# A three-layer interaction tower on one core: chunk 1's transfers on ScalarE's queue, the context product first, the last layer 2 in another bank

## The chip, the cores and the metric

The program runs on one core of a Trainium2 chip. The time is the device time of one execution in microseconds; three executions of the kernel before took 659.74, 657.54 and 658.29 us, so the median is 658.29 us. The engines are TensorE (PE in the profile; PEld is its weight load), VectorE (DVE), ScalarE (ACT), GpSimd (POOL) and SyncE (SP), which issues most DMA transfers.

## The reference

39 embedding tables are looked up for 512 samples, which gives e with 39 fields of 16 numbers for each sample. Three interaction layers follow, and then a small dense network on their outputs and on 16 context numbers:

```python
x0 = inputs; xk = inputs                       # (512, 39, 16)
for idx, (W, b) in enumerate(params):          # W: (39, fields of xk, 128)
    z = jnp.einsum('bhd,bkd,hks->bsd', x0, xk, W) + b[None, :, None]
    z = jax.nn.relu(z)
    if idx != n_layers - 1:
        half = z.shape[1] // 2
        xk = z[:, :half, :]; direct.append(z[:, half:, :])
    else:
        direct.append(z)
logit = jnp.sum(jnp.concatenate(direct, axis=1), axis=-1)      # (512, 256)
h = jnp.concatenate([logit, dense_ctx], axis=1)
h = jnp.maximum(h @ W_top1 + b_top1, 0.0)      # 272 -> 512
h = jnp.maximum(h @ W_top2 + b_top2, 0.0)      # 512 -> 256, then W_top3: 256 -> 1
```

## The kernel before

The 512 samples are cut into 16 chunks of 32 (`NCH`), so a chunk has N = 32 * 16 = 512 columns. For each chunk and layer, VectorE multiplies pairs of field rows (a product tile, `prod`, of 128 partitions and 2 x 512 numbers), and TensorE multiplies it with the weights and sums up in one PSUM bank: `z0` for layer 0 (written L0 here), `z1` for layer 1 (L1), `z2` for layer 2 (L2). L0 has 4 such groups in a chunk, L1 and L2 have 10 each.

Some groups are taken in two parts (`SPLIT`): ScalarE rounds the product to a short format (`high`), and the rest (`low`) is formed by GpSimd or, for the four groups in `THROUGH_PSUM`, by VectorE. TensorE then runs three cheaper passes (`sum_high`, `sum_low`) in place of the full-precision one (`sum_whole`).

The order is written out by hand. Stage i does L0 of chunk i, the first groups of L2 of chunk i-1, L1 of chunk i, and the rest of L2 of chunk i-1; a last stage (i = NCH) does L2 of chunk 15. Each engine runs its own list in order, and semaphores join the lists.

How a chunk's data comes in: GpSimd gathers its rows from the table (`gather`), 10 indirect DMAs for each chunk. Two copies of the gathered rows are stored to `x0_rows` in DRAM (`store_x0`); a DRAM to DRAM copy makes five more (`repeat_x0`); from there `x0base` (the second factor of L0, which ScalarE copies to the PSUM bank `base`), `spread0` (the first factors of L0) and three pieces of `spread` (the first factors of L1 and L2) are loaded. All of this is on SP's queue, except part of chunk 0's, which is on ScalarE's. The names `L261`, `L264` (stores), `L272` (repeat), `L283` (x0base), `L298` (spread0) and `L314` (spread) are those lines. The queue is one list: chunk 0's three spread loads are issued ahead of chunk 1's stores.

When a layer's sums are done, ScalarE takes relu of them out of the PSUM bank into `x1` or `x2` in the two arrangements that the next layer's products need (`copies`: six instructions, L464), and the other half of the rows into `r01` (L488, L502) or `r2` (L509), which VectorE reduces to the logits. For chunk 0 alone the copies are shared by ScalarE and VectorE (`first_copies`, four instructions on each, L472 and L616).

At the end, TensorE first does the context rows' product for the 512 hidden units (four matmuls, L763) ahead of the last stage, into `h1_sum`, whose first part is `z0`; after the last stage the logits' products are added to it (L769, L772), and ScalarE takes relu with the bias (L556). The second dense layer (L778), its relu (L560), the last product into `z0` (L783), a copy (L563) and the output transfer follow.

Of the kernel before, what the change touches and what calls it, by code (L numbers as in the profile page):

```python
# [8 lines left out]
P = 128  # L9
# [18 lines left out]
COPIES = 7  # L28

# [119 lines left out]
def tower_kernel(nc, ids, offsets, table, w0a, w0b, w1, w1_split, w2, w2_split, biases, wt1, bt1, wt2, bt2, wt3, ctxT, out):  # L149
    with ExitStack() as ctx:  # L150
# [45 lines left out]
        y_sb = sb("y_sb", [1, B])  # L196
        h1 = spread0[:, 0:H1 // P, :]
# [8 lines left out]
        h1_sum = (z0, x1[:, 0, :], x1[:, 1, :], z1)  # L206
        h2_sum = (base, x2[:, 0, :])

# [5 lines left out]
        bias_in = sem("bias_in")  # L214
        top_in = sem("top_in")
# [25 lines left out]
        h1_done = sem("h1_done")  # L241
        h1_ready = sem("h1_ready")
# [9 lines left out]
        def _(sp):  # L252
# [68 lines left out]
            sp.dma_start(bias_sb[:, :], biases).then_inc(bias_in, 16)  # L321
            sp.dma_start(w1_part, w1_split).then_inc(w1_in, 16)
# [33 lines left out]
            sp.wait_ge(y_ready, 1)  # L356
# [44 lines left out]
        def _(act):  # L401
# [4 lines left out]
            def store_first_again():  # L406

                act.wait_ge(gathered[0], 16 * GAT)
                first = x0_dram[0, F:F + 1, 0:1]
                act.dma_start(bass.AP(first.tensor, first.offset, [[D, P], [FPT * N, GAT - 1], [1, D]]),  # L410
                              gat[:, 0, 0:GAT - 1, :]).then_inc(x0_stored[0], 16)
                tail = x0_dram[0, F + FPT * (GAT - 1):F + FPT * (GAT - 1) + 1, 0:1]
                act.dma_start(bass.AP(tail.tensor, tail.offset, [[D, LAST], [1, D]]),
                              gat[0:LAST, 0, GAT - 1, :]).then_inc(x0_stored[0], 16)
# [52 lines left out]
            def first_copies(to, z, kind, layer, ready):  # L467

                act.wait_ge(mm_done, stage_end(0, kind))
# [35 lines left out]
            def relu2(c):  # L505
# [3 lines left out]
                act.activation(r2[:, :], z2[:, :], ACT.Relu, bias=bias_sb[:, 2:3]).then_inc(r2_ready, 1)  # L509
# [8 lines left out]
            store_first_again()  # L518
            load_first()
            take_base(0)  # L520
            for i in range(NCH + 1):
                if i >= 2:
                    for part in range(3):
                        relu1(i - 1, part)
                if i == NCH:
                    relu2(NCH - 2)
                for c, kind, gs in stages_of(i):
                    for g in gs:
# [6 lines left out]
                        if i == 1 and kind == "L0" and g == 1:  # L535
                            first_copies(x2, z1, "L1", 1, x2_ready)
                            relu1(0, 2)
                        if kind == "L0" and g == G0 - 1 and i >= 2:
                            relu2(i - 2)
# [13 lines left out]
            act.wait_ge(top_in, 16 * 7)  # L553
            for m in range(H1 // P):
                act.wait_ge(h1_done, m + 1)
# [297 lines left out]
```

## Time and profile before

| What | us |
|---|---|
| median of three executions | 658.29 |
| the profiled execution: time / span | 657.38 / 655.5 |
| PE busy | 608.5 (93%) |
| DVE busy | 550.0 (84%) |
| POOL busy | 537.1 (82%) |
| ACT busy | 409.3 (62%) |

The span is from the first to the last instruction of the profiled execution; 1.9 us lie around it. Stages 2 to 14 repeat every 36.35 us or so. The head (to about 80 us) and the tail (from about 610 us) are where the engines are seen waiting. "Idle before" in a row is the time in which the engine did nothing ahead of it, and the arrow names what ended that. A DMA row's duration is how long its queue took to issue it, not how long the bytes took.

### The profile page before, as it was taken

Reading aid. Unit: us, or ns where it says so; the run is one execution under the profiler, and the core shown is the slowest. Engines: PE = TensorE matmul, PEld = TensorE weight load, DVE = VectorE, ACT = ScalarE, POOL = GpSimd, SP = SyncE. Lnnn points to the kernel's source line nnn. Section 1 sums busy time; section 2 is a strip of 40 time slices with the busy share of each in tenths; the row PEclk is TensorE's granted clock in tenths of the full one; section 3 lists DMA queues with packets and bytes.
Section 4 is the critical chain, followed back from the end, with each engine's and each line's share of the span. In section 5 each row is a group of like instructions: output and inputs, shape, how many; then the busy total and the mean of one; then the engine's idle time right before and its main releaser. Section 6 shows DMA issues by size and latency. Waiting matters only on the chain.

```text
span 655.5 us, 6276 instructions
## 1 busy us (share of the span) xinstructions
PE 608.5 (93%) x1996; PEld 376.1 (57%) x1996; DVE 550.0 (84%) x620; ACT 409.3 (62%) x551; POOL 537.1 (82%) x325
## 2 busy tenths in 40 slices
PE   0178899999999999999999999999999999999998
PEld 0035466656666566656666566666566665655563
DVE  0376899898989898998989898999989898969750
ACT  2043758677676758576766757586776667584622
POOL 6786799898989899998989998999989895746530
PEclk9979899999999999999999999999999999999999
DMA  6687883838363645648374645547383745420000
GB/s 221 150 180 222 173 249 77 250 76 248 70 209 85 167 127 130 197 82 245 71 229 91 188 90 153 160 111 216 76 250 67 213 93 176 102 64 1 0 0 0
DMA packets 64043, 90.29 MB, mean 138 GB/s; under 512 B 46624, under 2 KB 49568, under 8 KB 60042
## 3 DMA queue, kind: packets, MB, share of 16 engines
q1 hardware_dynamic: 57402, 87.89, 49.5%
q0 software_dynamic: 5120, 1.29, 2.0%
q10 hardware_dynamic: 1488, 0.72, 0.4%
q8 instruction: 15, 0.25, 0.2%
q14 instruction: 18, 0.15, 0.1%
HBM read 87.31 MB, written 8.95 MB: 147 GB/s over the span
## 4 chain that ended last, share of the span: by engine, by line
PE 40%; POOL 36%; ACT 10%; issue 6%; DVE 5%; DMA 2%; SPq 0%; ACTq 0%; DVEq 0%
POOL low L378 29%; PE z L701 21%; PE z L718 10%; POOL gat L368 7%; PE z L733 6%; ACT x L464 6%; ACT high L444 2%; DVE prod L607 2%; ACT r L488 1%; DMA spread<-x_rows 1%; DVE x L616 1%; DVE prod L588 1%; DVE base L642 1%; DVE low L650 1%; PE x L778 1%
## 5 line engine op out<-in xcount | busy, mean ns | idle before, releaser
L378 POOL TENSOR_TENSOR low<-prod,high 128x1024 fp32r<-128x1024 f32 (+1 forms) x160 | 380.9, 2398 | 56.4 <-ACT high L444 55.1
L607 DVE TENSOR_TENSOR prod<-spread,x 128x1024 f32<-128x1024 f32 x256 | 308.1, 1214 | 35.3 <-ACT x L464 33.6
L701 PE MATMUL z<-prod,w_sb 128*128 128x512 f32 (+2 forms) x608 | 290.6, 598 | 37.3 <-DVE prod L588 32.8
L444 ACT ACTIVATE high<-prod 128x1024 fp32r<-128x1024 f32 (+1 forms) x160 | 167.8, 1058 | 124.0 <-DVE prod L607 99.8
L718 PE MATMUL z<-high,high_w_L 128*128 128x512 f32 (+1 forms) x448 | 203.7, 455 | 4.0 <-ACT high L444 2.8
L701 PEld LDWEIGHTS z<-prod,w_sb 128*128 128x128 f32 (+2 forms) x608 | 115.4, 190 | 122.8 <-issue 103.4
L368 POOL DMA_INDIRECT gat<-table_dram,index x160 | 155.5, 972 | 36.5 <-issue 33.9
L733 PE MATMUL z<-low,high_w_L 128*128 128x512 f32 (+1 forms) x448 | 182.1, 487 | 3.5 <-POOL low L378 1.9
L718 PE MATMUL z<-high,low_w_L 128*128 128x512 f32 (+1 forms) x448 | 179.0, 400 | 0.0
L464 ACT ACTIVATE x<-z,bias_sb 64x512 f32<-64x512 f32 (+1 forms) x180 | 116.3, 646 | 14.8 <-PE z L701 7.4
L733 PEld LDWEIGHTS z<-low,high_w_L 128*128 128x128 f32 (+1 forms) x448 | 82.8, 190 | 68.9 <-issue 44.7
L454 ACT ACTIVATE high<-base 128x512 fp32r<-128x512 f32 x128 | 75.5, 590 | 55.6 <-DVE base L642 55.2
L718 PEld LDWEIGHTS z<-high,high_w_L 128*128 128x128 f32 (+1 forms) x448 | 85.5, 191 | 42.2 <-issue 14.4
L718 PEld LDWEIGHTS z<-high,low_w_L 128*128 128x128 f32 (+1 forms) x448 | 85.5, 191 | 31.8 <-issue 14.2
L650 DVE TENSOR_TENSOR low<-base,high 128x512 fp32r<-128x512 f32 x128 | 87.8, 686 | 8.6 <-ACT high L454 8.3
L642 DVE TENSOR_TENSOR base<-spread,x 128x512 f32<-128x512 f32 x128 | 88.6, 692 | 2.3
L588 DVE TENSOR_TENSOR prod<-spread,base 117x1024 f32<-117x1024 f32 x64 | 65.4, 1082 | 15.0 <-DMA spread<-x_rows 8.4
L509 ACT ACTIVATE r<-z,bias_sb 128x512 f32<-128x512 f32 x16 | 11.0, 687 | 13.8 <-PE z L733 13.7
L628 DVE TENSOR_REDUCE logit<-r 128x32 f32<-128x512 f32 x16 | 10.9, 679 | 7.4 <-ACT r L509 7.4
L435 ACT ACTIVATE base<-x0base 117x512 f32<-117x512 f32 x16 | 9.6, 602 | 8.6 <-DMA x0base<-x_rows 8.2
L656 DVE TENSOR_TENSOR low_w_L<-spread,high_w_L 128x1792 fp32r<-128x1792 f32 (+1 forms) x2 | 3.7, 1888 | 10.1 <-DMA gat<-table_dram,index 10.1
L488 ACT ACTIVATE r<-z,bias_sb 64x512 f32<-64x512 f32 x16 | 11.0, 686 | 0.4
(37 smaller groups left out, 73.5 us busy)
## 6 DMA issues: line engine op xcount, KB each, us to landing
spread<-x_rows SPq DMA_DIRECT2D x15, 1792.0 KB, 7.1
spread<-x_rows SPq DMA_DIRECT2D x32, 768.0 KB, 11.0
spread<-x_rows SPq DMA_DIRECT2D x16, 1024.0 KB, 7.3
x_rows<-x_rows SPq DMA_DIRECT2D x16, 390.0 KB
x0base<-x_rows SPq DMA_DIRECT2D x47, 78.0 KB
gat<-table_dram,index POOLq DMA_INDIRECT x160, 3.7
x_rows<-gat SPq DMA_DIRECT2D x31, 72.0 KB, 2.3
wt_sb<-wt_dram SPq DMA_DIRECT2D x2, 512.0 KB, 17.4
```

The lines of the kernel that those rows point to most:

```text
L368: pool.indirect_dma_start(out=gat[0:rows, c % GBUF, j, :], out_offset=None, in_=table, in_offset=bass.IndirectOffsetOnAxis(ap=index[0:rows ...
L378: pool.tensor_tensor(low[0:rows, h, 0:k, :], prod[0:rows, slot(c, kind, g), 0:k, :], high[0:rows, h, 0:k, :].bitcast(F32), ALU.subtract).t ...
L444: act.activation(high[0:rows, split_slot(c, kind, g), 0:k, :], prod[0:rows, slot(c, kind, g), 0:k, :], ACT.Copy).then_inc(high_ready, 1)
L454: act.activation(high[0:rows, split_slot(c, kind, g), t, :], base[0:rows, :], ACT.Copy).then_inc(tile_high, 1)
L464: act.activation(to[at:end, tile, :], z[k:k + end - at, :], ACT.Relu, bias=bias_sb[k:k + end - at, layer:layer + 1]).then_inc(ready, 1)
L588: dve.tensor_tensor(prod[0:rows, slot(c, "L0", g), 0:k, :], spread0[0:rows, 2 * g:2 * g + k, :], base[0:rows, :].unsqueeze(1).to_broadcast ...
L607: dve.tensor_tensor(prod[0:rows, slot(c, kind, g), :, :], spread[0:rows, c % 2, g, :].unsqueeze(1).to_broadcast([rows, k, N]), x[0:rows, : ...
L642: dve.tensor_tensor(base[0:rows, :], spread[0:rows, c % 2, g, :], x[0:rows, t, :], ALU.mult).then_inc(tile_prod, 1)
L650: dve.tensor_tensor(low[0:rows, h, t, :], base[0:rows, :], high[0:rows, h, t, :].bitcast(F32), ALU.subtract).then_inc(tile_low, 1)
L701: last = pe.matmul(z[:, :], w[0:rows, at + j, :], prod[0:rows, slot(c, kind, g), j, :], start=g == 0 and j == 0, stop=closes and j == k - 1)
L718: pe.matmul(z[:, :], v[kind][0:rows, at + j, :], high[0:rows, h, j, :], start=g == 0 and j == 0 and v is high_w, stop=False)
L733: last = pe.matmul(z[:, :], high_w[kind][0:rows, at + j, :], low[0:rows, h, j, :], start=False, stop=closes and j == k - 1)
```

## The change

1. Chunk 1's stores, its repeat, its x0base and its spread0 load leave SP's queue and are issued by ScalarE: the two stores and the repeat ahead of ScalarE's relu copies of L0 of chunk 0, the loads behind them. `spread` of chunk 1 stays with SP.
2. The context product is TensorE's first work, into the banks of `x1` and `x2`; VectorE adds the bias and keeps the result in `ctx_part`. Its three small loads move to the front of SP's queue. At the end VectorE adds `ctx_part` to the hidden sums, and ScalarE's relu reads the result.
3. L2 of chunk 15 sums in `z0` in place of `z2`, so it need not wait until ScalarE has read chunk 14's sums; the hidden layer's first part takes `z2`.
4. The relu copies of L1 of chunk 15 are shared by ScalarE and VectorE; ScalarE's relu of chunk 14's L2 moves behind group 2 of the last stage, and VectorE's reduction of it behind group 5.
5. The dense layers' other weights are loaded in stage 4 (`TOP_AT`), not ahead of chunk 2's stores.
6. The last product is done in two halves of 256 columns in two banks, each copied on its own.

```diff
-        h1_sum = (z0, x1[:, 0, :], x1[:, 1, :], z1)
+        h1_sum = (z2, x1[:, 0, :], x1[:, 1, :], z1)
         h2_sum = (base, x2[:, 0, :])
+        ctx_sum = (x1[:, 0, :], x1[:, 1, :], x2[:, 0, :], x2[:, 1, :])
+        y_sum = (z0[0:1, 0:B // 2], z1[0:1, 0:B // 2])
+
+        def sum_bank(c, kind):
+            return z0 if kind == "L2" and c == NCH - 1 else {"L0": z0, "L1": z1, "L2": z2}[kind]
...
+            sp.dma_start(wt1c_sb[:, :], wt1[2 * P:, :]).then_inc(ctx_in, 16)
+            sp.dma_start(ctx_sb[:, :], ctxT).then_inc(ctx_in, 16)
+            sp.dma_start(bt1_sb[:, :], bt1).then_inc(ctx_in, 16)
...
-            store_x0(1)
-            load_base(1)
-            repeat_x0(1)
-            load_spread0(1)
             for p in range(len(PIECES)):
                 load_spread(1, p)
-            sp.dma_start(wt1_sb[:, :, :], wt1[0:2 * P, :].rearrange("(t p) n -> p t n", p=P)).then_inc(top_in, 16)
-            sp.dma_start(wt1c_sb[:, :], wt1[2 * P:, :]).then_inc(top_in, 16)
-            sp.dma_start(bt1_sb[:, :], bt1).then_inc(top_in, 16)
-            sp.dma_start(wt2_sb[:, :, :], wt2.rearrange("(t p) n -> p t n", p=P)).then_inc(top_in, 16)
-            sp.dma_start(bt2_sb[:, :], bt2).then_inc(top_in, 16)
-            sp.dma_start(wt3_sb[:, :], wt3).then_inc(top_in, 16)
-            sp.dma_start(ctx_sb[:, :], ctxT).then_inc(top_in, 16)
             store_x0(2)
...
+                if i == TOP_AT:
+                    sp.dma_start(wt1_sb[:, :, :], wt1[0:2 * P, :].rearrange("(t p) n -> p t n", p=P)).then_inc(top_in, 16)
+                    sp.dma_start(wt2_sb[:, :, :], wt2.rearrange("(t p) n -> p t n", p=P)).then_inc(top_in, 16)
+                    sp.dma_start(bt2_sb[:, :], bt2).then_inc(top_in, 16)
+                    sp.dma_start(wt3_sb[:, :], wt3).then_inc(top_in, 16)
...
+            def store_x0(c, copies):
+
+                act.wait_ge(gathered[c], 16 * GAT)
+                for n in copies:
+                    first = x0_dram[c, n * F:n * F + 1, 0:1]
+                    act.dma_start(bass.AP(first.tensor, first.offset, [[D, P], [FPT * N, GAT - 1], [1, D]]),
+                                  gat[:, c, 0:GAT - 1, :]).then_inc(x0_stored[c], 16)
+                    at = n * F + FPT * (GAT - 1)
+                    tail = x0_dram[c, at:at + 1, 0:1]
+                    act.dma_start(bass.AP(tail.tensor, tail.offset, [[D, LAST], [1, D]]),
+                                  gat[0:LAST, c, GAT - 1, :]).then_inc(x0_stored[c], 16)
+
+            def repeat_second():
+
+                act.wait_ge(x0_stored[1], 64)
+                row = x0_dram[1, 0:1, 0:1]
+                to = x0_dram[1, 2 * F:2 * F + 1, 0:1]
+                act.dma_start(bass.AP(to.tensor, to.offset, [[N, F], [F * N, COPIES - 2], [1, N]]),
+                              bass.AP(row.tensor, row.offset, [[N, F], [0, COPIES - 2], [1, N]])
+                              ).then_inc(x0_copied[1], 16)
+
+            def load_second():
+
+                for j in range(DPT):
+                    row = x0_dram[1, (F - j * T0) % F:(F - j * T0) % F + 1, 0:1]
+                    act.dma_start(x0base[j * F:(j + 1) * F, :], bass.AP(row.tensor, row.offset, [[N, F], [1, N]])
+                                  ).then_inc(base_in, 16)
+                act.wait_ge(prod_done, PROD_NUMBER[0, "L0", G0 - 1])
+                act.wait_ge(x0_copied[1], 16)
+                row = x0_dram[1, 0:1, 0:1]
+                act.dma_start(spread0[:, :, :].rearrange("p t n -> p (t n)"),
+                              bass.AP(row.tensor, row.offset, [[N, P], [1, T0 * N]])).then_inc(spread0_in, 16)
...
+            def shared_copies(c, to, z, kind, layer, ready):
+
+                act.wait_ge(mm_done, stage_end(c, kind))
+                if c >= 1:
+                    ringed, tiled = products_of(c - 1, "L1" if kind == "L0" else "L2", range(G1))
+                    act.wait_ge(prod_done, ringed)
+                    if tiled:
+                        act.wait_ge(tile_prod, tiled)
                 for tile in range(2):
                     for q in range(tile, FPT, 2):
...
+                if i == NCH:
+                    shared_copies(i - 1, x2, z1, "L1", 1, x2_ready)
+                    relu1(i - 1, 2)
+                elif i >= 2:
                     for part in range(3):
                         relu1(i - 1, part)
-                if i == NCH:
-                    relu2(NCH - 2)
                 for c, kind, gs in stages_of(i):
...
-                        first_copies(x1, z0, "L0", 0, x1_ready)
+                        store_x0(1, (0, 1))
+                        repeat_second()
+                        shared_copies(0, x1, z0, "L0", 0, x1_ready)
                         relu0(i, 2)
+                        load_second()
             relu2(NCH - 1)
...
+                act.wait_ge(h1_summed, m + 1)
+                act.activation(h1[:, m, :], h1[:, m, :], ACT.Relu).then_inc(h1_ready, 1)
...
+            dve.wait_ge(ctx_in, 16 * 3)
+            for m in range(H1 // P):
+                dve.wait_ge(ctx_done, m + 1)
+                dve.tensor_scalar(ctx_part[:, m, :], ctx_sum[m], bt1_sb[:, m:m + 1], 0.0, ALU.add, ALU.add)
...
+            for m in range(H1 // P):
+                dve.wait_ge(h1_done, m + 1)
+                dve.tensor_tensor(h1[:, m, :], h1_sum[m][:, :], ctx_part[:, m, :], ALU.add).then_inc(h1_summed, 1)
...
+                if kind == "L2" and c == NCH - 1 and gs[0] == 0:
+                    pe.wait_ge(r0_ready, NCH)
+                elif gs[0] == 0 and c >= 1:
...
+            pe.wait_ge(ctx_in, 16 * 3)
+            for m in range(H1 // P):
+                pe.matmul(ctx_sum[m], wt1c_sb[:, m * P:(m + 1) * P], ctx_sb[:, :],
+                          start=True, stop=True).then_inc(ctx_done, 1)
...
-            pe.wait_ge(top_in, 16 * 7)
-            pe.wait_ge(r0_ready, NCH)
-            pe.wait_ge(r1_ready, NCH)
-            for m in range(H1 // P):
-                pe.matmul(h1_sum[m][:, :], wt1c_sb[:, m * P:(m + 1) * P], ctx_sb[:, :], start=True, stop=False)
             for c, kind, gs in stages_of(NCH):
                 sum_stage(c, kind, gs)
 
+            pe.wait_ge(top_in, 16 * 4)
+            pe.wait_ge(r2_ready, NCH - 1)
+            pe.wait_ge(r1_ready, NCH)
...
+                for n in range(2):
+                    last = pe.matmul(y_sum[n], wt3_sb[:, k:k + 1], h2[:, k, n * B // 2:(n + 1) * B // 2],
+                                     start=(k == 0), stop=(k == H2 // P - 1))
+                    if k == H2 // P - 1:
+                        last.then_inc(y_done, 1)
```

How ScalarE's list stands at the end of L0 of chunk 0, before:

```order
L444 ACTIVATE high<-prod 117x1024
L472 ACTIVATE x<-z,bias_sb 32x512 x4
L488 ACTIVATE r<-z,bias_sb 64x512
L444 ACTIVATE high<-prod 128x1024
L454 ACTIVATE high<-base 128x512
L444 ACTIVATE high<-prod 128x1024
L454 ACTIVATE high<-base 128x512
L444 ACTIVATE high<-prod 128x1024
L454 ACTIVATE high<-base 128x512
```

ScalarE's list there now, from the same rounding (`high`) of L0's split group on (`x_rows<-gat` are the stores, `x_rows<-x_rows` the repeat, `x<-z` the relu copies into `x1`, `x0base` and `spread` chunk 1's loads):

```order
L474 ACTIVATE high<-prod 117x1024
L418 DMA x_rows<-gat 128x9x16
L422 DMA x_rows<-gat 96x16
L418 DMA x_rows<-gat 128x9x16
L422 DMA x_rows<-gat 96x16
L430 DMA x_rows<-x_rows 39x5x512
L507 ACTIVATE x<-z,bias_sb 32x512 x4
L523 ACTIVATE r<-z,bias_sb 64x512
L438 DMA x0base<-x_rows 39x512 x3
L443 DMA spread<-x_rows 128x3584
L474 ACTIVATE high<-prod 128x1024
L484 ACTIVATE high<-base 128x512
```

Five transfers stand ahead of the four relu copies, and four behind them, ahead of the first rounding of L1. The repeat waits until the stores have landed (`x0_stored`, 64).

SP's list from chunk 0's repeat on, before:

```order
L272 DMA x_rows<-x_rows 39x5x512
L314 DMA spread<-x_rows 128x1x1536 x2
L314 DMA spread<-x_rows 128x1x2048
L261 DMA x_rows<-gat 128x9x16
L264 DMA x_rows<-gat 96x16
L261 DMA x_rows<-gat 128x9x16
L264 DMA x_rows<-gat 96x16
L283 DMA x0base<-x_rows 39x512 x3
L272 DMA x_rows<-x_rows 39x5x512
L298 DMA spread<-x_rows 128x3584
L314 DMA spread<-x_rows 128x1x1536 x2
L314 DMA spread<-x_rows 128x1x2048
```

SP's list there now (the second group of `spread` rows is chunk 1's, the stores behind it are chunk 2's):

```order
L282 DMA x_rows<-x_rows 39x5x512
L324 DMA spread<-x_rows 128x1x1536 x2
L324 DMA spread<-x_rows 128x1x2048
L324 DMA spread<-x_rows 128x1x1536 x2
L324 DMA spread<-x_rows 128x1x2048
L271 DMA x_rows<-gat 128x9x16
L274 DMA x_rows<-gat 96x16
L271 DMA x_rows<-gat 128x9x16
```

Chunk 1's stores, x0base, repeat and spread0 are gone from it, so its three spread pieces stand straight behind chunk 0's.

TensorE's list where the last stage begins, before (`ctx_sb,wt1c_sb` is the context product):

```order
L701 MATMUL z<-prod,w_sb 128x512 x2
L733 MATMUL z<-low,high_w_L 128x512 x2
L763 MATMUL z<-ctx_sb,wt1c_sb 128x512
L763 MATMUL x<-ctx_sb,wt1c_sb 128x512 x2
L763 MATMUL z<-ctx_sb,wt1c_sb 128x512
L718 MATMUL z<-high,high_w_L 128x512
L718 MATMUL z<-high,low_w_L 128x512
L718 MATMUL z<-high,high_w_L 128x512
L718 MATMUL z<-high,low_w_L 128x512
```

TensorE's list there now:

```order
L756 MATMUL z<-prod,w_sb 128x512 x2
L788 MATMUL z<-low,high_w_L 128x512 x2
L773 MATMUL z<-high,high_w_L 128x512
L773 MATMUL z<-high,low_w_L 128x512
L773 MATMUL z<-high,high_w_L 128x512
L773 MATMUL z<-high,low_w_L 128x512
L773 MATMUL z<-high,high_w_L 128x512
L773 MATMUL z<-high,low_w_L 128x512
```

The four context matmuls between chunk 14's and chunk 15's L2 are gone.

## Rows read from the trace of the kernel before

**Rows 1.** The page, chain that ended last: share of the span by engine.

```profile
PE 40%; POOL 36%; ACT 10%; issue 6%; DVE 5%; DMA 2%; SPq 0%; ACTq 0%; DVEq 0%
```

**Rows 2.** Chain of waits, head: start us, us, engine and line.

```profile
57.40 4.54 issue
```

**Rows 3.** Timeline of VectorE, head: start us, us, instruction, idle before it.

```profile
38.21 3.13 DVE L616 TENSOR_SCALAR x<-z,bias_sb 32x512 f32<-32x512 f32 x4 [3.31 <-PE z L701]
41.37 2.35 DVE L607 TENSOR_TENSOR prod<-spread,x 128x1024 f32<-128x1024 f32 x2
...
61.94 4.08 DVE L588 TENSOR_TENSOR prod<-spread,base 117x1024 f32<-117x1024 f32 x4 [6.28 <-issue]
```

**Rows 4.** Timeline of ScalarE, head.

```profile
38.14 2.65 ACT L472 ACTIVATE x<-z,bias_sb 32x512 f32<-32x512 f32 x4 [4.55 <-PE z L701]
40.81 0.68 ACT L488 ACTIVATE r<-z,bias_sb 64x512 f32<-64x512 f32 x1
```

**Rows 5.** Timeline of SP's queue, head: start us, us to issue.

```profile
35.97 0.85 SPq L261 DMA_DIRECT2D x_rows<-gat  x1
...
50.17 1.13 SPq L283 DMA_DIRECT2D x0base<-x_rows  x3
51.35 0.85 SPq L272 DMA_DIRECT2D x_rows<-x_rows  x1
55.16 0.34 SPq L298 DMA_DIRECT2D spread<-x_rows  x1
```

**Rows 6.** Chunk 0's spread loads by line: ns to issue, first and last start.

```profile
L314 SPq DMA_DIRECT2D spread<-x_rows x3: 590/597/602, 34.0 to 35.3; - x3
DMA to landing us min/median/max: 6.3/8.9/13.1
```

**Rows 7.** A stretch: us, five engines' busy time, PEclk, DMA share, GB/s.

```profile
36.00:40.00 4.00, 2.10 (x6) 0.76 (x4) 1.72 (x3) 1.81 (x3) 2.93 (x5) 1.00 1.01 257
```

**Rows 8.** Landing of gathers issued at 29.6-30.9, 36.2-40.0 and 68.0-79.0 us.

```profile
DMA to landing us min/median/max: 3.7/4.0/4.3
...
DMA to landing us min/median/max: 8.2/8.9/9.4
...
DMA to landing us min/median/max: 2.3/3.3/7.6
```

**Rows 9.** Timeline of queues: stores of chunk 0, then of chunk 3.

```profile
18.59 0.42 ACTq L410 DMA_DIRECT2D x_rows<-gat  x1
...
22.11 0.74 SPq L283 DMA_DIRECT2D x0base<-x_rows  x2
...
108.19 0.39 SPq L261 DMA_DIRECT2D x_rows<-gat  x1
...
113.63 0.83 SPq L272 DMA_DIRECT2D x_rows<-x_rows  x1
```

**Rows 10.** Chain of waits, tail, all TensorE.

```profile
617.13 1.05 PE z L763 x2
...
620.76 3.24 PE z L718 x8
...
634.64 0.93 PE z L718 x4
635.57 1.72 PE z L701 x4
637.29 0.47 PE z L733 x2
...
651.49 1.82 PE z L783 x4
```

**Rows 11.** Timelines of ScalarE and of GpSimd, tail.

```profile
611.68 4.01 ACT L464 ACTIVATE x<-z,bias_sb 64x512 f32<-64x512 f32 x6 [0.72 <-DVE prod L607]
...
618.88 4.71 POOL L378 TENSOR_TENSOR low<-prod,high 128x1024 fp32r<-128x1024 f32 x2 [5.47 <-ACT high L444]
```

**Rows 12.** A stretch of the last stage.

```profile
620.70:625.00 4.30, 4.30 (x13) 3.38 (x13) 4.27 (x6) 0.60 (x1) 2.89 (x2) 0.60 0.00 0
```

More of the change, by code:

```diff
@@ L28 @@
 COPIES = 7
+TOP_AT = 4
 DELTAS = (F + 1) // 2
@@ L196, in tower_kernel @@
         y_sb = sb("y_sb", [1, B])
+        ctx_part = sb("ctx_part", [P, H1 // P, B])
         h1 = spread0[:, 0:H1 // P, :]
@@ L214, in tower_kernel @@
         bias_in = sem("bias_in")
+        ctx_in = sem("ctx_in")
+        ctx_done = sem("ctx_done")
         top_in = sem("top_in")
@@ L241, in tower_kernel @@
         h1_done = sem("h1_done")
+        h1_summed = sem("h1_summed")
         h1_ready = sem("h1_ready")
@@ L404, in split_weights @@
                                ).then_inc(high_w_ready, 1)
[L406 to L414, printed above, removed]
+            def store_x0(c, copies):
[8 more added lines that the diff above has]
+                                  gat[0:LAST, c, GAT - 1, :]).then_inc(x0_stored[c], 16)
@@ L508, in relu2 @@
                     act.wait_ge(summed2, c)
-                act.activation(r2[:, :], z2[:, :], ACT.Relu, bias=bias_sb[:, 2:3]).then_inc(r2_ready, 1)
+                act.activation(r2[:, :], sum_bank(c, "L2")[:, :], ACT.Relu, bias=bias_sb[:, 2:3]).then_inc(r2_ready, 1)
             act.wait_ge(w0_folded, 1)
@@ L517, in _ @@
             act.wait_ge(bias_in, 16)
-            store_first_again()
+            store_x0(0, (1,))
             load_first()
@@ L535, in _ @@
                         if i == 1 and kind == "L0" and g == 1:
-                            first_copies(x2, z1, "L1", 1, x2_ready)
+                            shared_copies(0, x2, z1, "L1", 1, x2_ready)
                             relu1(0, 2)
                         if kind == "L0" and g == G0 - 1 and i >= 2:
+                            relu2(i - 2)
+                        if i == NCH and g == 2:
                             relu2(i - 2)
@@ L548, in _ @@
                     if kind == "L0" and i == 0:
[L549 removed]
+                        store_x0(1, (0, 1))
+                        repeat_second()
+                        shared_copies(0, x1, z0, "L0", 0, x1_ready)
                         relu0(i, 2)
+                        load_second()
             relu2(NCH - 1)
[L553 removed]
+            act.wait_ge(top_in, 16 * 4)
             for m in range(H1 // P):
[L555 to L557 removed]
+                act.wait_ge(h1_summed, m + 1)
+                act.activation(h1[:, m, :], h1[:, m, :], ACT.Relu).then_inc(h1_ready, 1)
             for m in range(H2 // P):
@@ L595, in wait_factors @@
                 if g == 0:
-                    dve.wait_ge(ready, (2 + FPT) * (c + 1) + 2)
+                    dve.wait_ge(ready, (2 + FPT) * (c + 1) + (4 if kind == "L2" and c == NCH - 1 else 2))
                 for p, (at, _) in enumerate(PIECES):
@@ L609, in product, with shared_copies @@
                                   x[0:rows, :, :], ALU.mult).then_inc(prod_done, 1)
-            def first_copies(to, z, kind, layer, ready):
-                dve.wait_ge(mm_done, stage_end(0, kind))
+            def shared_copies(c, to, z, kind, layer, ready):
+                dve.wait_ge(mm_done, stage_end(c, kind))
+                if c >= 1:
+                    ringed, tiled = products_of(c - 1, "L1" if kind == "L0" else "L2", range(G1))
+                    dve.wait_ge(prod_done, ringed)
+                    if tiled:
+                        dve.wait_ge(tile_prod, tiled)
                 for tile in range(2):
@@ L667, in _ @@
             for i in range(NCH + 1):
+                if i == NCH:
+                    shared_copies(i - 1, x2, z1, "L1", 1, x2_ready)
                 for c, kind, gs in stages_of(i):
@@ L682, in _ @@
                             sum01(c)
-                        if kind == "L2" and g == 3 and c >= 1:
+                        if kind == "L2" and g == (5 if c == NCH - 1 else 3) and c >= 1:
                             sum2(c - 1)
@@ L739, in sum_stage @@
                 closing = stage_end(c, kind)
-                if gs[0] == 0 and c >= 1:
+                if kind == "L2" and c == NCH - 1 and gs[0] == 0:
+                    pe.wait_ge(r0_ready, NCH)
+                elif gs[0] == 0 and c >= 1:
                     pe.wait_ge({"L0": r0_ready, "L1": r1_ready, "L2": r2_ready}[kind], c)
@@ L782, in _ @@
                 pe.wait_ge(h2_ready, k + 1)
-                last = pe.matmul(z0[0:1, :], wt3_sb[:, k:k + 1], h2[:, k, :],
-                                 start=(k == 0), stop=(k == H2 // P - 1))
-            last.then_inc(y_done, 1)
+                for n in range(2):
+                    last = pe.matmul(y_sum[n], wt3_sb[:, k:k + 1], h2[:, k, n * B // 2:(n + 1) * B // 2],
+                                     start=(k == 0), stop=(k == H2 // P - 1))
+                    if k == H2 // P - 1:
+                        last.then_inc(y_done, 1)
 def layer_rows(w, gs):
```

23 lines of the change are left out of this document (9 added, 14 removed).

## Prediction

> **What bounds the kernel now.** I read the chain that ended last first. Over the whole span TensorE has 40% of it and GpSimd 36% [rows 1]: in the 13 steady stages the roundings' low parts and the matmuls set the pace, and this change moves nothing there. So what it is worth lies in the head and the tail, and there I read the chain in order of time and then each engine's timeline.
>
> In the head the chain has a hole. From 57.40 us, when chunk 1's `base` is there, nothing on it runs for 4.54 us [rows 2] until VectorE starts chunk 1's L0 at 61.94, after 6.28 us idle [rows 3]. What is late is spread0: it is issued at 55.16, behind the repeat (51.35), which waited for the stores, whose landing shows as the x0base load at 50.17 [rows 5]. The stores were issued from 35.97 on, behind chunk 0's three spread loads in the same queue; the last of those, issued at 35.3, landed 13.1 us later, at 48.4 [rows 6].
>
> In the tail the chain is TensorE without a gap: 3.63 us of context product (617.13 to 620.76), then chunk 15's L2 until 637.76 (637.29 + 0.47), then the dense layers [rows 10].
>
> **The change part by part.**
>
> *Chunk 1's transfers.* Call S the moment at which chunk 1's stores have landed. ScalarE's list is in order, so behind its wait for S stand: the repeat's issue (0.85 on SP [rows 5]), the four relu copies of L0 (2.65 [rows 4]), and through them everything of chunk 0's L1: VectorE's products wait for all eight copies, TensorE and GpSimd wait for the products. VectorE would start L1 at S + 0.85 + 2.65 + 0.05 = S + 3.55, where it did at 41.37 [rows 3]. The delay is S - 37.8. What it buys is the hole, 4.54, since spread0 then comes in while L1 runs. The head as a whole changes by S - 42.4: it loses when S is later than 42.4.
>
> Before, S was 50.17. Now the stores are issued when the last gather has landed, 30.9 + 3.7 = 34.6 [rows 8], in a queue of their own. S is bounded by two rows. Quiet, from first issue to the repeat behind the landed stores, chunk 3 took 113.63 - 108.19 = 5.44 us [rows 9]: S = 40.0, head -2.4. But these are not quiet: chunk 0's spread loads start 0.5 us ahead of them and keep the 16 DMA engines at a share of 1.01 from 36 to 40 [rows 7] and land at 48.4 [rows 6]; if the stores come through only behind them, S = 48.4 + about 1.8 (that is how long before's took behind the same loads) = 50.2, head +7.8. Between these I go by the nearest case of another queue's small pieces under the same loads: a gather issued at 36.2 to 40.0 took 8.9 us to land, and 3.3 in a calmer stretch [rows 8], although it came on its own queue. A store of two copies is about 2,500 pieces of 64 bytes (2 x (9 x 128 + 96)), a gather is 128. A second queue has not spared even the gather; twenty times as many pieces will hardly slip through. I take S = 49.7, a little ahead of the upper bound because they are queued 1.4 us sooner: delay 11.9, less 4.5, head **+7.3**.
>
> The Trainium skill speaks against this part too: "DMA: Bandwidth & Descriptors", section "Issuing engines are not separate DMA queues", says that transfers issued by different engines run on the same 16 DMA engines, so that another issuer saves only issue time. The gathers' 8.9 us agree.
>
> ScalarE then also holds three x0base issues (1.13) and waits for the repeat, 55.16 - 51.35 = 3.8 us from its issue [rows 5], so about S + 3.8. It is done with copies, relu (0.68 [rows 4]) and these issues at S + 5.3, so this wait is hidden; the first rounding of L1 is wanted at S + 3.55 + 2.4, just behind. But SP, which only waits for the repeat, issues chunk 1's spread loads at S + 3.8, about 2 us ahead of spread0. Three such loads took 48.4 - 34.0 = 14.4 us to land [rows 6]; spread0 behind all of them would land near S + 3.8 + 14.4 + 4 = S + 22, and VectorE wants it at 57.40 + (S - 37.8) = S + 19.6. So 0 to 2.5 us; I take **+0.4**, since the queues differ and some of it will come between.
>
> *Loads and context product at the start.* Three more issues on SP (0.5 us each) push the L1 and L2 weights back by 1.4 us; ScalarE's next step after rounding them is chunk 0's second store at 18.59 [rows 9], which waits for the gathers, so they are free. Neither TensorE nor VectorE has a product to work on before that store has landed: the four matmuls and four bias additions cost 0. If that cover were thinner than it looks, 1 us at most. The dense weights in stage 4 (1 MB) are hidden by the stage's own DMA pauses; VectorE waits for no load in steady stages. Taking them from the head frees SP's queue only for chunk 2's transfers, for which nothing waits. 0.
>
> *The tail.* TensorE can start chunk 15's L2 at 617.13 instead of 620.76; the other bank means no wait for ScalarE's read of chunk 14's sums. Its work there is 6 groups of high passes at 0.93, 6 of low at 0.47, and 4 whole at 1.72 [rows 10] = 15.3 us. It took 17.0 before, because the first eight high passes took 3.24 and not 1.86: the granted clock in 620.7 to 625 is 0.60, that is, in part the lower level of 1.2 GHz, right behind the context matmuls of 16 rows [rows 12]. With these gone I expect 2.4 GHz throughout. Now the feeders are late: the copies start at 611.68 [rows 11]; shared they take VectorE's 3.13 [rows 3] and not 4.01, so products come 0.88 sooner; and the rounding no longer stands behind the relu of chunk 14's sums, some 0.7 (0.68 for a like one [rows 4]). So GpSimd begins 1.6 sooner, at 617.3 where it was 618.88. Its first two low parts take 4.71 [rows 11]: ready at 622.0. By then TensorE has done high, high, low, high (3.3 us) and waits. From 622.0 it has 12.0 us left: end 634.0, plus 0.2 for short stalls: 634.2 against 637.76, **-3.5**. Bounds: -5.4 with no stall (617.1 + 15.3), -1.5 if the stalls bring back the low clock.
>
> *The dense layers.* The first logit products (3.4 us) still cover ScalarE's and VectorE's last relu and sum. A DVE addition of 0.69 now stands ahead of the relu for each of four parts; they follow at 0.86, the matmuls that read them at 0.86 too, and the last is wanted 2.6 us after the second layer starts: 0. The last product in halves lets the first half be copied under a quarter of 1.82 [rows 10]: between 0 and -0.45, **-0.2**.
>
> Sum: 7.3 + 0.4 - 3.5 - 0.2 = +4.0. The profiled execution takes 657.38 (span 655.5 and 1.9 around it), so it becomes 661.4; on the median of 658.29, **662.3 us**.
>
> **The rivals.**
>
> A, the stores come through early. If each DMA engine serves the two queues side by side, S is between 40.0 (unhindered) and 43.5: two queues with one copy each had theirs stored in 22.11 - 18.59 = 3.5 us [rows 9], and at half the engines' time that part comes twice, 34.6 + 5.44 + 3.5. Head -2.4 to +1.1, tail -3.7: 652.2 to 655.7, faster; it decides from S below 44. For it: those two queues did not hold one another up. Against it: the gathers' landing. The Trainium skill has a rule that would give this: "DMA: Bandwidth & Descriptors", section "Queues, rings and completion order", says that each DMA engine goes round between the queues and takes a whole packet of some 9 to 17 descriptors from one before it switches. By it the 156 store pieces of an engine would need some 9 to 17 turns against 24 rows of the spread loads, and the time would be about 655, an estimate. No row here shows how many 64-byte pieces one turn takes.
>
> B, they are held up once, as a gather is, and then run: 34.6 + 5.44 + (8.9 - 3.3) = 45.6, head +3.2, with the tail's -3.7 and +0.2: 658.0, no change.
>
> C, the tail pays less: TensorE's new stalls bring the low clock back, or the shared copies start later because VectorE is not free. Tail -1.7 and the head as forecast: 664.3, slower.
>
> **How the numbers follow.** Forecast 0.55, A 0.24, B 0.14, C 0.07. What can be told from no change is 0.3%, 2.0 us: faster below 656.3, slower above 660.3. Faster is A, 0.24 and a little of B: 0.25. Slower is the forecast and C less an edge: 0.60. Same: 0.15. The forecast's own range is 660 to 664.5. The range for all, 653.5 to 665.5, leaves out the lower part of A and extreme spread0 delays.
>
> **What would show it.** Right: the four relu copies on ScalarE start near 50.5 us, not 38; VectorE idles from 41 to about 53; the hole before chunk 1's L0 is gone or under 2 us, and these products start near 69.7; the last stage's first high pass follows chunk 14's last low pass at once, the granted clock there is 1.00, and the stage is 3 to 4 us shorter. Wrong: ScalarE's repeat issued before 44 us. Then the head gains or stands even, and the time is that of A or B.

## The result and the profile after

Against its own 20 runs of the kernel before (median 658.80 us), the changed kernel takes 661.15 us (660.28 to 663.19): ratio 1.0045 (3.0 us), 95% interval 1.0034 to 1.0056, slower by less than half a per cent. The two medians differ by 2.35 us. Its profiled execution takes 660.79 us with a span of 658.8, where before had 657.38 and 655.5: +3.3 in the span.

ScalarE's timeline in the head after the change (start us, us, engine and line, operation; ACTq is the issue of a transfer; then the idle time before it):

```profile
34.05 0.39 ACTq L418 DMA_DIRECT2D x_rows<-gat  x1
34.48 0.83 ACTq L422 DMA_DIRECT2D x_rows<-gat  x1
35.34 0.68 ACTq L418 DMA_DIRECT2D x_rows<-gat  x1
36.05 6.22 ACTq L422 DMA_DIRECT2D x_rows<-gat  x1
49.16 0.90 ACTq L430 DMA_DIRECT2D x_rows<-x_rows  x1
50.11 0.64 ACT L507 ACTIVATE x<-z,bias_sb 32x512 f32<-32x512 f32 x1 [16.75 <-DMA x_rows<-gat]
...
53.14 0.37 ACTq L443 DMA_DIRECT2D spread<-x_rows  x1
```

The stores' fourth issue alone takes 6.22 us, to 42.27. Then ScalarE waits, and the repeat is issued at 49.16: that is S, forecast at 49.7. The relu copies that stood at 38.14 [rows 4] are at 50.11, 16.75 us of idle time before them, put down to the stores. VectorE, in its own timeline:

```profile
38.74 3.13 DVE L662 TENSOR_SCALAR x<-z,bias_sb 32x512 f32<-32x512 f32 x4 [4.42 <-PE z L756]
52.79 2.35 DVE L648 TENSOR_TENSOR prod<-spread,x 128x1024 f32<-128x1024 f32 x2 [10.92 <-ACT x L507]
...
68.84 1.22 DVE L629 TENSOR_TENSOR prod<-spread,base 117x1024 f32<-117x1024 f32 x1 [1.75 <-ACT base L465]
```

Its own four copies are not held up (38.74, and 38.21 in [rows 3]). Its first product of chunk 0's L1 comes at 52.79, 11.42 us later than in [rows 3] (forecast 11.9), and chunk 1's L0 at 68.84 and not at 61.94: +6.90 (forecast +7.7). In front of it stand 1.75 us, ended by `base`, and not 6.28. From there on nothing changes: the stages have the lengths of before, and chunk 15's L1 copies start at 618.58, again +6.90 against [rows 11].

The tail after the change, in three views: the timeline (ScalarE's and VectorE's shared copies, GpSimd's first two low parts), the chain of waits (start us, us, engine, what), and the stretches of the last stage (columns as in [rows 12]: the clock is the third number from the right).

```profile
618.58 2.65 ACT L507 ACTIVATE x<-z,bias_sb 32x512 f32<-32x512 f32 x4 [0.72 <-DVE prod L648]
618.59 3.13 DVE L662 TENSOR_SCALAR x<-z,bias_sb 32x512 f32<-32x512 f32 x4
...
624.14 4.75 POOL L385 TENSOR_TENSOR low<-prod,high 128x1024 fp32r<-128x1024 f32 x2 [3.83 <-ACT high L474]
```

```profile
627.91 0.61 ACT high L484
628.52 0.04 issue
628.57 0.74 PE z L773 x2
...
640.83 0.47 PE z L788 x2
641.30 0.86 PE z L828 x2
...
655.04 1.83 PE z L843 x8
```

```profile
620.00:628.50 8.50, 7.46 (x26) 4.12 (x24) 8.34 (x11) 5.77 (x8) 4.67 (x3) 1.00 0.00 1
628.50:634.00 5.50, 5.43 (x17) 3.16 (x18) 5.47 (x8) 1.67 (x3) 2.50 (x2) 1.00 0.00 0
```

The copies take 3.13 us in place of 4.01 and GpSimd begins 5.56 us behind their start in place of 7.20 [rows 11], 1.64 sooner (forecast 1.6). From the start of the copies to the end of the last stage it was 637.76 - 611.68 = 26.08 us; it is 641.30 - 618.58 = 22.72: -3.36 (forecast -3.5). The clock is 1.00 throughout where [rows 12] had 0.60. The chain no longer runs through TensorE alone: ahead of 628.57 TensorE waited for a rounding of ScalarE's, and that one for VectorE's `base`.

So 6.90 - 3.36 - 0.2 (the last product in halves) = +3.3, the whole of the difference of the spans.

### The profile page after: what moved, and what is told of

Read it like the earlier page. It is cut to its first block and busy times, and to the rows that moved or that the text cites. A ratio compares the mean times of both kernels' runs of the same rounds, so it can differ in the third digit from the quotient of the medians.

```text
span 658.8 us, 6297 instructions
## 1 busy us (share of the span) xinstructions
PE 610.5 (93%) x2000; PEld 375.5 (57%) x2000; DVE 558.9 (85%) x632; ACT 408.2 (62%) x550; POOL 536.6 (81%) x325
## 5 line engine op out<-in xcount | busy, mean ns | idle before, releaser
L494 ACT ACTIVATE x<-z,bias_sb 64x512 f32<-64x512 f32 (+1 forms) x174 | 112.5, 646 | 14.0 <-PE z L756 7.4
L507 ACT ACTIVATE x<-z,bias_sb 32x512 f32<-32x512 f32 x12 | 7.7, 642 | 17.7 <-DMA x_rows<-gat 16.7
L811 PE MATMUL x<-ctx_sb,wt1c_sb 16*128 16x512 f32 x8 | 7.2, 1076 | 7.8 <-DMA bt_sb<-bt_dram 7.8
```

The source lines that it names most:

```text
L494: act.activation(to[at:end, tile, :], z[k:k + end - at, :], ACT.Relu, bias=bias_sb[k:k + end - at, layer:layer + 1]).then_inc(ready, 1)
```

## The experiments

Every ratio is to the kernel before, run beside it on the same chip. Stage 0 below is the time from chunk 0's first L0 product to chunk 1's; tail is the time from the start of chunk 15's L1 copies to the end of the last stage. These two leave out how early the first gathers came in one execution.

### The two parts apart: e1 and e2

e1 is the kernel after with chunk 1's transfers back on SP, e2 the kernel before with only these moved to ScalarE.

```diff
 e1, SP's list                        e1, ScalarE's list
+ store_x0(1)                        - store_x0(1, (0, 1)); repeat_second()
+ load_base(1); repeat_x0(1)           shared_copies(0, x1, z0, ...)
+ load_spread0(1)                      relu0(i, 2)
  load_spread(1, p)                  - load_second()
```

> The changed kernel with chunk 1's stores, x0base, repeat and spread0 back on SP's queue and ScalarE's relu copies of L0 with no wait ahead of them; all else as changed. Theory (the head costs 6.9 us, the tail gives 3.5 to 3.8): ScalarE's copies at about 38.5 us, chunk 1's L0 at about 62, the last stage as in the changed kernel, total 3.6 us under the kernel before, ratio 0.9945. Rival (the early context product or the weights pushed back cost something in the head too): chunk 1's L0 starts later than 62.5 and the ratio is above 0.997.

> The kernel before with chunk 1's stores, x0base, repeat and spread0 issued by ScalarE as in the changed kernel, and nothing else (context product, banks, shared copies and dense weights as before). Theory: L1 of chunk 0 starts near 52.8, chunk 1's L0 near 68.8, everything behind is later by 6.9 us, ratio 1.0105. Rival (part of the delay is made by loads that the change moved off SP's queue and is given back or made worse without that): the shift at chunk 15 differs from the shift at chunk 1's L0 by more than 1 us.

e1: 654.17 us, ratio 0.994 [0.992, 0.996]. e2: 663.98, ratio 1.0088 [1.0055, 1.0121]. The two parts have opposite signs, and each shows without the other. e1's stage 0 is 32.74 us, e2's 39.09, before's 33.52, after's 40.35. e1's tail is 22.72, the same as after's to the hundredth. e2's ratio, 5.8 us, agrees with its stage 0, +5.57. But its profiled execution (666.40 us, the longest of its seven) is dearer than that: its next stage is 39.77 us long and not 38.33, and its tail 27.68 and not 26.08. Its shift against the kernel before grows with that from 6.07 us at chunk 1's L0 to 7.21 at chunk 15, by more than the 1 us that the rival named. In e12, the same kernel profiled again, it is 7.31 and 7.17, so the rival does not hold. Both stretches are taken up below (e9 to e12).

### Where the head's time goes: e3, e7, e8, e4

e3 holds SP's second and third spread loads of chunk 0 back until the stores have landed, so that these meet one load and not three. e7 leaves the stores' issues where the change put them, but takes the copies out from behind the wait.

```diff
 e3, SP                               e7, ScalarE
  load_spread(0, 0)                    store_x0(1, (0, 1))
+ sp.wait_ge(x0_stored[1], 64)       + shared_copies(0, x1, z0, ...); relu0(i, 2)
  load_spread(0, 1)                    repeat_second()
  load_spread(0, 2)                  - shared_copies(0, x1, z0, ...); relu0(i, 2)
```

> The changed kernel, but SP waits for chunk 1's stores to have landed before it issues chunk 0's second and third spread load; the first stays ahead. Theory (the stores are late because the spread loads keep the DMA engines busy): ScalarE issues the repeat near 42.5 us and not 49.2, and its copies of L0 start near 43.4. The repeat then lies behind two spread loads, so ScalarE is held in its wait for it to about 52 and the gain is partly lost: total about level with the kernel before, ratio 0.998 to 1.002. Rival (ScalarE's queue is slow with the stores whatever else moves): the repeat is still issued at 48 or later.

> The kernel after, but on ScalarE the relu copies and the relu of chunk 0's L0 come ahead of the wait for the stores (the stores' issues still ahead of them). Theory of two parts: 6.2 us of the delay are the queue's full ring, which blocks the issue until 42.3, and 7 us are the wait for the landing. So the copies start at 42.3 and VectorE's L1 at 45.0 instead of 52.8; but ScalarE then waits from 46 to 49.15 and on to 53.1 ahead of its first rounding, so chunk 1's L0 starts only 2 to 3 us sooner than in the kernel after (68.84), at about 66.5: ratio 1.001. Rival 1 (the copies alone were what mattered): L0 starts at 61 to 62, ratio 0.994. Rival 2 (the issue is not blocked by the ring but by what ScalarE waits for, so that with the copies next they start before 40): the same 61 to 62 or sooner.

e3: 658.71 us, 1.0002 [0.998, 1.002]. ScalarE's timeline in it:

```profile
42.32 0.90 ACTq L432 DMA_DIRECT2D x_rows<-x_rows  x1
43.27 0.64 ACT L509 ACTIVATE x<-z,bias_sb 32x512 f32<-32x512 f32 x1 [10.46 <-DMA x_rows<-gat]
...
50.58 0.37 ACTq L445 DMA_DIRECT2D spread<-x_rows  x1
51.00 1.06 ACT L476 ACTIVATE high<-prod 128x1024 fp32r<-128x1024 f32 x1 [4.38 <-DMA x_rows<-x_rows]
```

S is 42.3 and not 49.2: the two further loads cost the stores 6.8 us. Only 4.1 of them come back in stage 0 (36.26), because the wait for the repeat, hidden in the kernel after, now stands in front of the first rounding (51.00, 4.38 us idle before it).

e7: 659.85 us, 1.0035 [1.0014, 1.0057], stage 0 38.13. ScalarE, then VectorE in it:

```profile
36.59 6.01 ACTq L422 DMA_DIRECT2D x_rows<-gat  x1
42.65 2.65 ACT L507 ACTIVATE x<-z,bias_sb 32x512 f32<-32x512 f32 x4 [9.10 <-issue]
...
49.49 0.89 ACTq L430 DMA_DIRECT2D x_rows<-x_rows  x1
...
53.14 0.37 ACTq L443 DMA_DIRECT2D spread<-x_rows  x1
53.56 1.06 ACT L474 ACTIVATE high<-prod 128x1024 fp32r<-128x1024 f32 x1 [7.55 <-DMA x_rows<-x_rows]
```

```profile
45.33 2.35 DVE L648 TENSOR_TENSOR prod<-spread,x 128x1024 f32<-128x1024 f32 x2 [2.81 <-ACT x L507]
...
48.32 1.21 DVE L648 TENSOR_TENSOR prod<-spread,x 128x1024 f32<-128x1024 f32 x1
55.27 0.69 DVE L696 TENSOR_TENSOR low<-base,high 128x512 fp32r<-128x512 f32 x1 [5.74 <-ACT high L484]
...
67.21 4.08 DVE L629 TENSOR_TENSOR prod<-spread,base 117x1024 f32<-117x1024 f32 x4 [1.75 <-ACT base L465]
```

The blocked issue is there without any wait behind it: 6.01 us, and the copies start at 42.65, 4.5 later than in [rows 4]. VectorE starts L1 at 45.33, 7.5 us sooner than in the kernel after, but two products later it stands still for 5.74 us, since the roundings it needs are behind ScalarE's wait for S (49.49, as late as after's 49.16) and for the repeat (53.14). 7.5 us of earlier start are worth 2.2 in stage 0. In time, where 1.001 was expected, the interval just leaves that out and cannot tell e7 from the kernel after; rival 1 (0.994) and rival 2 (copies before 40) are both out.

e4 and e8 are e1 with chunk 1's stores in SP's own queue, ahead of chunk 0's third spread load (e4), or ahead of the second and third (e8).

```diff
 e4                                   e8
  load_spread(0, 0)                    load_spread(0, 0)
  load_spread(0, 1)                  + store_x0(1)
+ store_x0(1)                          load_spread(0, 1)
  load_spread(0, 2)                    load_spread(0, 2)
- store_x0(1)                        - store_x0(1)
```

> As e1 (all of chunk 1's transfers on SP's queue), but chunk 1's stores are issued between chunk 0's second and third spread load and not behind the third. Theory (only the place of the stores against the 1 MB loads counts, not the queue): the stores land near 46, spread0 is issued near 52, the hole before chunk 1's L0 shrinks from 4.5 to about 1.5 us, third piece a little late but still hidden: ratio to before 0.9905 (3.6 us from the tail, 2.7 from the head). Rival (the third piece comes too late for L1's sixth group, or the repeat waits behind it anyway): head as before or worse, ratio 0.9945 or above.

> The kernel of e1 with chunk 1's stores issued on SP after chunk 0's first spread load and ahead of the second and third (e4 had them ahead of the third only). Theory: the stores land at about 42.5 to 43.5 (42.3 in e3 with one spread load ahead of them), the repeat and spread0 follow 3 us sooner than in e4, and the hole before chunk 1's L0 is gone; what the second and third loads lose shows as VectorE's waits for spread inside chunk 0's L1, 2 to 4 us where e4 had 2.2. Chunk 1's L0 starts between 59 and 61 (60.16 in e4): ratio 0.9905, 0.989 to 0.992. Rival (the stores hold the later loads up by their whole 8 us): L0 starts at 64, ratio 0.997.

e4: 651.99 us, 0.9906 [0.987, 0.994]. e8: 652.45, 0.9918 [0.989, 0.995]. SP's queue in e4, then in e8:

```profile
39.04 4.53 SPq L274 DMA_DIRECT2D x_rows<-gat  x1
43.62 0.54 SPq L324 DMA_DIRECT2D spread<-x_rows  x1
46.05 1.13 SPq L293 DMA_DIRECT2D x0base<-x_rows  x3
47.23 0.83 SPq L282 DMA_DIRECT2D x_rows<-x_rows  x1
53.02 0.34 SPq L308 DMA_DIRECT2D spread<-x_rows  x1
```

```profile
36.65 3.58 SPq L274 DMA_DIRECT2D x_rows<-gat  x1
40.27 1.19 SPq L324 DMA_DIRECT2D spread<-x_rows  x2
42.76 1.14 SPq L293 DMA_DIRECT2D x0base<-x_rows  x3
43.94 0.83 SPq L282 DMA_DIRECT2D x_rows<-x_rows  x1
54.03 0.34 SPq L308 DMA_DIRECT2D spread<-x_rows  x1
```

The stores land at 46.1 behind two loads and at 42.8 behind one. In e8 this is lost again: its repeat, issued 3.3 us sooner, now stands behind two loads, and spread0 is issued at 54.03, 10.1 us after it, where e4 has 5.8. VectorE in e8 also waits 2.85 us for the second load. So e8's expectation, that the hole would be gone, failed. Stage 0 is 31.36 in e4 and 32.42 in e8 (32.05 in e11): e4's place is 0.7 to 1.1 us better in these profiles, which the two ratios can't confirm. e4 beats both kernels: by its ratio 6.2 us less than before (3.8 to 8.6), and about 9 less than after.

### The tail taken apart: e5 and e6

e5 is e1 with chunk 15's copies on ScalarE alone again. e6 is e1 with the four context matmuls issued once more ahead of the last stage.

```diff
 e5                                   e6, TensorE
- if i == NCH: shared_copies(...)    + for m in range(H1 // P):
                                     +     pe.matmul(x1[:, 0, :], wt1c_sb[...],
                                     +               ctx_sb[:, :], ...)
                                       for c, kind, gs in stages_of(NCH):
```

> The kernel of e1 (the new tail, chunk 1's transfers on SP), but chunk 15's L1 copies are ScalarE's alone again, six of them for 4.01 us, as in the kernel before. Theory: the last stage's pace is that of its feeders, which hang on these copies, so it ends 0.9 us later than in e1 (633.78), at about 634.7: 1.0014 of e1, 0.9955 of the kernel before. Rival (the gain of the tail is all TensorE's, by its earlier start and its clock): the end does not move, 0.994.

> The kernel of e1 with the four context matmuls issued once more right ahead of the last stage, into a bank that nobody reads then (their result is not used; the output is the same). TensorE idles some 5 us in e1's last stage, so 3.63 us of added work ahead of it could vanish there. Theory: it does not vanish, since these matmuls of 16 rows leave TensorE at the low clock, as before: granted clock about 0.6 in the 4 us behind them, and the stage ends 1.5 to 3 us later than in e1: 635.3 to 636.8, ratio 0.9965 to 0.9985. Rival (clock stays at 1.00, the feeders hide the rest): 0 to 0.7 us later, ratio 0.994 to 0.995.

e5: 655.62 us, 0.9956 [0.993, 0.998]; tail 23.50, so the shared copies are worth 0.78. e6: 656.25 us, 0.9978 [0.996, 1.000]; tail 24.52. The chain of e6 in the last stage, and a stretch of it:

```profile
617.01 3.63 PE x L822 x8
620.63 2.06 PE z L774 x8
622.69 0.47 PE z L789 x2
...
635.61 0.47 PE z L789 x2
636.08 0.86 PE z L831 x2
```

```profile
620.63:625.00 4.37, 4.37 (x19) 3.40 (x19) 4.37 (x7) 1.72 (x3) 1.32 (x2) 1.00 0.00 0
```

For e6 the theory had the right size and a wrong reason. The clock stays at 1.00: eight high passes take 2.06 us here and 3.24 in [rows 10]. Yet the stage ends 1.80 us later than in e1, because TensorE, starting at 620.63, works 15.45 us without a stall (15.3 was the count of its work), while in e1 it could begin 3.6 us sooner and lost half of that again in waits for products and roundings. So a product of 3.63 us ahead of the stage costs 1.80 with no help from the clock. The rival would have hidden all but 0.7.

### Whether the low clock belongs to the kernel: e9 to e12

These are the kernels before, e6, e8 and e2, unchanged, each profiled once more.

> The kernel before, unchanged, profiled once more. Its first profile had a granted clock of 0.57 from 621 to 625 behind the context product and a last stage of 17.0 us; e6, with the same four context matmuls at the same place, had 1.00 and 15.45 us. Theory (the low clock there belongs to the order of this kernel's work): 0.5 to 0.65 again in these 4 us and a last stage of 17.0. Rival (whether it falls is decided by the execution, not by the kernel): 1.00 there, a stage of 15.5 and a span 1.5 us shorter, about 654.

> The kernel of e6, unchanged, profiled once more. Theory (the kernel's order decides): granted clock 1.00 behind the added context matmuls again, last stage 15.4 to 15.6 us. Rival (the execution decides): a stretch of 3 to 6 us at the low clock can show there, stage 16.5 to 18.

> The kernel of e8, unchanged, profiled once more. Its first profile had a low clock (0.72) from 82 to 88 and a stage of 39.74 us there, against 38.32 in e4. Theory (the kernel's order decides): the same 39.7. Rival (the execution decides): 38.3 and a span 1.4 us shorter, about 650.7.

> The kernel of e2, unchanged, profiled once more. Its first profile had low clocks at 88 to 94 (stage of 39.77 us) and from 625 to 634. Theory (the kernel's order decides): both again, span 664. Rival (the execution decides): one or both absent, span 661 to 663.

| kernel | stage after chunk 1's L0, 1st / 2nd profile | tail, 1st / 2nd | span, 1st / 2nd |
|---|---|---|---|
| before, e9 | 38.33 / 38.31 | 26.08 / 27.62 | 655.5 / 658.1 |
| e6, e10 | 38.32 / 38.32 | 24.52 / 24.51 | 653.6 / 654.8 |
| e8, e11 | 39.74 / 38.31 | 22.72 / 22.70 | 652.1 / 651.0 |
| e2, e12 | 39.77 / 38.31 | 27.68 / 24.51 | 664.3 / 661.1 |

A stretch of the last stage of the one kernel e2, first profile and then second:

```profile
627.00:633.00 6.00, 6.00 (x12) 3.47 (x11) 5.97 (x9) 1.63 (x3) 3.77 (x2) 0.50 0.00 0
```

```profile
627.90:632.00 4.10, 4.10 (x18) 3.24 (x18) 4.07 (x6) 0.60 (x1) 2.90 (x2) 1.00 0.00 0
```

Granted clock 0.50, that is the lower level of 1.2 GHz throughout, in one execution, and 1.00 in the other. e8's long stage is the same thing (0.72 from 82 to 88, and 1.00 in e11). For e8 and e2 the rival holds: the execution decides. In e9 the kernel before has a low clock in its tail again (0.65 from 620 to 624, 0.50 from 624 to 628), but for longer than expected: the last stage takes 18.07 us and not 17.0. e6's expectation held, 1.00 again in e10. With two profiles each that does not show that the kernel decides there, and e12 has the last stage and the context product of the kernel before at 1.00. What it hangs on stays open. The second profiles differ in stage 0 too, by 0.04 us for the kernel before, 0.1 for e6, 0.4 for e8 and most for e2: 39.09 and 40.70, with S at 48.3 and 49.6. What is shown is the size: the old tail is 24.51 at full clock and up to 3.2 us longer when the clock falls, the new one was 22.70 to 22.72 at a full clock in all seven profiles of it (after, e1, e3, e4, e7, e8, e11).

## Why the prediction was right

*The stores come through late.* Held. S was taken as 49.7 and is 49.2 (48.3, 49.5 and 49.6 in e2, e7 and e12). The runs show what it hangs on: 42.3 with one load beside the stores (e3), 42.8 and 46.1 with one or two ahead of them in the same queue (e8, e4), 49.5 to 51.2 with three ahead (six profiles, [rows 5] among them), and 48.3 to 49.6 with three in another queue. Counted from chunk 0's first product, a queue of their own won 0.8 us on average over standing last (19.4 to 21.0 us against 20.7 to 21.8).

Why so little shows in the DMA records of the profile after. From 38 to 40 us 1,122 records of ScalarE's queue go through beside 86 of SP's. But from 41 to 46 it is 179 beside 164 (162 beside 168 in e7 and in e12): about one piece of 64 bytes for each row of the loads. The last 1,176 follow from 46 to 48.2, when the loads run out (31 records). The prediction did not know this; it went by a gather's delay and came close with an argument that did not count turns. Its reason for putting S just under the upper bound, "queued 1.4 us sooner", was misread. SP's own issues in the kernel before were as blocked, and [rows 5] leaves these two out:

```profile
36.86 5.94 SPq L264 DMA_DIRECT2D x_rows<-gat  x1
...
43.37 4.64 SPq L264 DMA_DIRECT2D x_rows<-gat  x1
```

The last issue ended there at 48.01 and after the change at 42.27, 5.7 us sooner, and the stores still landed only 1.0 us sooner.

Rival A would have needed S below 44, and it is out. So is what the prediction worked out from the Trainium skill's "DMA: Bandwidth & Descriptors", section "Queues, rings and completion order", an estimate of about 655: by that rule the DMA engine takes 9 to 17 descriptors of one queue before it turns to the next. From 41 to 46 us it was about one, and the measurement decides. The same page of the Trainium skill, section "Issuing engines are not separate DMA queues", says that another issuer saves only issue time, and these 0.8 us agree. Rival B's 45.6 is out too.

*The delay reaches everything behind it.* Held: 11.42 against 11.9. One cause was left out: not all of it is the wait. The issue of the stores itself blocks ScalarE until 42.3, and in e7, with the copies out from behind the wait, they were still 4.5 us late. The sum came out because this time lies wholly inside the wait for S; with S below 42.3 it would not have.

*The hole is bought back.* Held, 4.5 of the delay. The term for a late spread0, +0.4, was 0: it is `base` that ended VectorE's last wait of 1.75 us, and the next chunk's L0 (107.16) has no wait at all. The two terms of the head together were 7.7 and came to 6.90.

*The tail.* The sum held, -3.36 against -3.5, and e1 shows it alone. The stall that ended last was not the one forecast: GpSimd's low parts were done at 628.89 and wanted at 629.31, and what TensorE waited for was the rounding, done at 628.52, of one of the groups in `THROUGH_PSUM`, whose product and low part are VectorE's. The two lie within 0.4 us of each other, so the end came out right, in part by luck. The make-up of the sum was argued from one profile. I gave 1.7 to the clock (the first eight high passes explain 1.38 of it by the prediction's own numbers) and the rest to the earlier start. In before's profile the split is 1.56 (26.08 - 24.52) of clock and 1.80 of the rest, of which 0.78 are the shared copies (e5). But the 1.56 is what the clock took in that one execution; in e9 it was 3.1, and in e12, the same tail, 0. So "with these gone I expect 2.4 GHz" described what followed, not a sure cause, and e1's ratio (2.5 to 5.4 us) is too wide to say how much of it the median execution got. Rival C, new stalls that bring the low clock back, did not occur.

*What was costed at nothing.* The early context product and its additions, the dense weights in stage 4, the additions ahead of the relu: none shows as a loss. There was even a little that I had not seen: with the new tail and the old head stage 0 is 32.7 to 33.2 us (e1, e5, e6, e10), where it is 33.5 in both profiles of the kernel before. In e1 spread0 is issued sooner (54.30, and 55.16 in [rows 5]), but in e5, e6 and e10 it is issued as late after chunk 0's first product as in e9 (26.15 to 26.19 us, and 26.18). So the cause stays open; which of the moved loads gives this was not tried.

The sum of +4.0 stands against +3.4 in the profiled executions, and against +0.45%, 3.0 us, in the ratio. No term is off by more than 0.5 us.

## What to carry to other kernels

Before a transfer with a wait behind it is moved to another engine's queue, read what stands behind it in that engine's list: ScalarE stood idle for the landing (16.75 us here), and the issue of many small pieces alone took 6.22 of it. If the transfer is late because bigger ones are ahead, a new queue may win little, and its place in the old queue wins more; but look at the next transfer in the chain, which then meets the ones that were let pass. A low TensorE clock seen in one profile should be seen in a second before a gain is put down to it.

## What the runs showed of the hardware

The last of four store issues on ScalarE took 6.22 us (5.36 in e2, 6.01 in e7, 6.13 in e12, 3.83 in e3 with one load beside it) where the same issue of the first copy took 0.83: ScalarE did nothing else meanwhile. On SP it took 4.64 in the kernel before, and 4.53 and 3.58 in e4 and e8. It is time of the issuer, not of the transfer: in e7 the copies start at its end, 42.65, and the stores land at 49.49. SP had nothing else to issue that did not wait for the stores anyway. In the four profiles with the stores on ScalarE beside three loads the issue ended when 1,231 to 1,241 of the 2,496 pieces had been moved, so with about 1,260 still to go each time. That fits a queue that holds about so many and blocks its issuer until there is room; it is an inference from these counts, and no run changed the number of pieces.

In the kernel after TensorE stood idle for 15.44 us ahead of chunk 0's L1 and began again at a granted clock of 0.50 (54 to 58 us), with 1.00 from 60 on. The forecast did not have this. It cost nothing that shows: the delay of 11.42 less the 4.53 bought back is the whole shift of 6.90 to within 0.01.

The granted clock of one unchanged kernel differed between executions in short stretches: 0.50 or 1.00 for 6 us in the tail of e2, 0.72 or 1.00 at 82 to 88 in e8. Such stretches cost 1.4 to 3.2 us in a profile, at the most about as much as the tail's part of this change gave.
